# A tiled adapter with per-sequence experts: tile 0's transposes in two banks, one bias copy moved up, one weight load on another queue

## Chip, cores and metric

One core of one Trainium2 chip. The time is device microseconds of one execution; medians are over several executions. Engines: TensorE (PE), VectorE (DVE), ScalarE (ACT), GpSimd (POOL) and SyncE (SP).

## What is computed

64 sequences of 64 rows and 512 columns (float32) go through an adapter. Each sequence chooses one of three experts by an index. The reference, cut:

```python
h = jnp.einsum('bsh,bhk->bsk', x, W_down[stream]) + b_down[stream]   # 512 -> 256
h = gelu(h)
h = jnp.einsum('bsk,bkh->bsh', h, W_up[stream]) + b_up[stream]       # 256 -> 512
h = x + h
out = layernorm(h) * ln_w[stream] + ln_b[stream]
```

## The kernel before

**Tiles.** Sequences are sorted by expert on the chip and packed in pairs: 33 tiles of 128 rows. `t` is the tile; buffers go by `t` modulo 2 (`PAR`), 4 (`DEEP`, `YBANKS`) or 8 (`FAR`).

**Split products.** Each float32 operand is split into a high part (a cast to float32r by ScalarE) and a low part (operand minus high part, by VectorE or GpSimd). A product is three matmul passes: high by high, high by low, low by high. So a tile takes these steps: PE transposes x into a PSUM bank (`transpose_x`, 4 transposes); ACT casts it (`x_hi`), DVE subtracts (`x_lo`); PE runs `down` (12 matmuls); DVE adds the bias (`down_bias`), ACT does `gelu`; PE transposes g, ACT and DVE split it (`g_hi`, `g_lo`); PE runs `up` (6 matmuls of 512 columns). POOL makes x plus the up bias (`add_bias`, into `xb`), ACT copies that into the PSUM bank `y_ps` of the tile (`seed`) before `up` adds to it; for tile 0 DVE adds it afterwards (`add_first`). Then follow the norm's steps (DVE `stats`, `mean_var`, `variance`, `scale`; POOL `power`, `shift`; ACT `rescale`) and the two stores.

**Weights.** W_up lies in three slots of two halves, each half 128x512. SP asks for each (`load_w_up`), ACT casts it (`wu_high`), and the low part (`w_up_low(slot, half)`) is made by DVE for (0,0), (0,1), (1,0) and (2,1), by POOL for (1,1) and (2,0). For tiles 1 and 2 `up` runs high by high, then low g by high weight, then high g by low weight, and waits for the low parts of DVE and POOL before the last.

**Order.** There is no planner: every engine has its own instruction order, written out by hand for the first tiles, then a loop. SP, before the change: first halves of tiles 0 and 1, W_up slot 0, tile 2, slot 1, tiles 3 and 4, slot 2, tile 5, the norm's weights, tile 6, the norm's biases, then the rest. ACT asks for the second halves of tiles 0 and 1. PE's head: transposes of tile 0, first pass of `down` 0, transposes of tile 1, other passes of `down` 0, `down` 1, transposes of g 0, of tile 2, `up` 0, then from tile 1 on g transposes, `down` of the next tile, x transposes, `up`. The bias rows come out of PSUM banks too: `y_ps[0]` holds those of expert 0 until ACT has copied them (`keep_up_bias(0)`, which signals `bu_ready`).

The lines that matter: 416 to 422 (POOL's order), 545 to 570 (ACT's), 786 to 805 (DVE's), 906 to 929 and 968 (PE).

Of the kernel before, what the change touches and what calls it, by code (L numbers as in the profile page):

```python
# [21 lines left out]
P = 128  # L22
# [3 lines left out]
def adapter_program(nc, x, itok, w_down, b_down, w_up, b_up, ln_w, ln_b, out):  # L26
# [34 lines left out]
    LATE = 10  # L61

    CLOSER = 6

    DVE_LOWS, POOL_LOWS = (2, 3, 4), (0, 1, 2)

# [3 lines left out]
    with ExitStack() as ctx:  # L70
# [6 lines left out]
        def sem(name):  # L77
            return ctx.enter_context(nc.semaphore(name))
# [109 lines left out]
        xT_ready = sem("xT_ready")  # L188
        xhi_ready = sem("xhi_ready")
        xlo_ready = sem("xlo_ready")  # L190
        h_ready = sem("h_ready")
        hb_ready = sem("hb_ready")
        g_ready = sem("g_ready")
# [22 lines left out]
        def ds(start, n):  # L216
            return bass.ds(start, n)
# [6 lines left out]
        def landed_count(t, c):  # L224

            return 32 * (t // FAR + 1) if isinstance(t, int) else t * (32 // FAR) + 32 - (32 // FAR) * (c % FAR)
# [30 lines left out]
        def load_w_up(eng, slot, e):  # L257

            for k in range(KB):
                part = w_up[ds(e, 1), k * P:(k + 1) * P, :].rearrange("a p n -> p (a n)")  # L260
                eng.dma_start(wu[:, slot, k, :], part).then_inc(wu_in[slot * KB + k], 16)
# [15 lines left out]
        def _(sp):  # L277
# [34 lines left out]
            def slot_expert(slot, reg):  # L312

                return sp.snap(reg, min_val=0, max_val=E - 1 - slot) + slot
# [12 lines left out]
            sp.reg_load(io_regs, io_table[0:1, 6:9])  # L327
            load(2, 2, rows(io_regs[:2]))
            load_w_up(sp, 1, slot_expert(1, io_regs[2]))
            sp.reg_load(head_regs[:3], io_table[0:1, 9:12])  # L330
            load(3, 3, rows(head_regs[:2]))
            load(4, 4, entries(4, 0, 2))
            load_w_up(sp, 2, slot_expert(2, head_regs[2]))
            load(5, 5, entries(5, 0, 2))
            sp.dma_start(lnw_rows[:], rows_of(ln_w, P)).then_inc(lnw_in, 16)
            load(6, 6, entries(6, 0, 2))
# [23 lines left out]
        def _(pool):  # L360
# [24 lines left out]
            def add_bias(t, c):  # L385

                e = expert_of(pool, t)
                pool.wait_ge(x_in[c % FAR], landed_count(t, c))
                if isinstance(t, int) and t == DEEP:
                    pool.wait_ge(seeded_first, 1)  # L390
                elif from_tile(t, DEEP):
                    pool.wait_ge(seeded, t - DEEP)
                pool.tensor_tensor(xb[:, c % DEEP, :], x_sb[:, c % FAR, :], bu_rows[:, ds(e * H, H)],  # L393
                                   ALU.add).then_inc(xb_ready, 1)
# [19 lines left out]
            pool.wait_ge(bu_last_ready, 1)  # L414
            pool.wait_ge(bu_ready, E - 1)
            add_bias(0, 0)
            add_bias(1, 1)
            pool.wait_ge(wu_lo_ready, KB)
            add_bias(2, 2)
            w_up_low(pool, 1, 1).then_inc(wu_lo_pool, 1)  # L420
            add_bias(3, 3)
# [33 lines left out]
        def _(act):  # L455
# [27 lines left out]
            def x_hi(t, c):  # L483

                act.wait_ge(xT_ready, t + 1)
                act.copy(xT_hi[:, c % PAR, :], xT_ps[c % PAR][:]).then_inc(xhi_ready, 1)  # L486
# [11 lines left out]
            def seed(t, c):  # L498

                act.wait_ge(xb_ready, t + 1)  # L500
                if from_tile(t, YBANKS):
                    act.wait_ge(scaled_ready, t - YBANKS + 1)
                act.copy(y_ps[c % YBANKS][:], xb[:, c % DEEP, :]).then_inc(seeded, 1)  # L503
# [41 lines left out]
            wd_high(2)  # L545
            keep_up_bias(0)
            keep_up_bias(1)
            x_hi(0, 0)
            keep_down_bias(0)
            keep_down_bias(1)  # L550
            x_hi(1, 1)
# [7 lines left out]
            wu_high(1, 1)  # L559
            g_hi(1, 1)  # L560
            seed(1, 1)
            x_hi(3, 3)
            gelu(2, 2)
            wu_high(2, 0)
            g_hi(2, 2)
            wu_high(2, 1)
            seed(2, 2)
            x_hi(4, 4)
            gelu(3, 3)
            seed(3, 3)  # L570
# [58 lines left out]
        def _(dve):  # L629
# [80 lines left out]
            def x_lo(t, c):  # L710

                dve.wait_ge(xhi_ready, t + 1)
                dve.tensor_tensor(xT_lo[:, c % PAR, :], xT_ps[c % PAR][:], xT_hi[:, c % PAR, :].bitcast(F32),  # L713
                                  ALU.subtract).then_inc(xlo_ready, 1)
# [70 lines left out]

            dve.wait_ge(up_spread, E)
            dve.tensor_copy(bu_rows[:, (E - 1) * H:E * H], y_ps[E - 1][:]).then_inc(bu_last_ready, 1)  # L787
            x_lo(0, 0)
            x_lo(1, 1)
            dve.wait_ge(bd_ready, len(bd_banks))  # L790
            down_bias(0, 0, first_experts[0])
# [72 lines left out]
        def _(pe):  # L864
# [41 lines left out]
            def transpose_x(t, c):  # L906
# [3 lines left out]
                    mm = pe.transpose(xT_ps[c % PAR][:, k * P:(k + 1) * P], x_sb[:, c % FAR, k * P:(k + 1) * P], ident[:])  # L910
                mm.then_inc(xT_ready, 1)

            def down(t, c, e, passes=(0, 1, 2)):

                w0 = e * (KH * BN)
                pe.wait_ge(xhi_ready, t + 1)
                h = h_ps[c % PAR]
                products = (xT_hi, wd_hi), (xT_hi, wd_lo), (xT_lo, wd_hi)
                for x_half, w_half in [products[i] for i in passes]:
                    if isinstance(t, int) and t == 0 and w_half is wd_lo:  # L920
                        pe.wait_ge(wd_lo_ready, E)
                    if x_half is xT_lo:
                        pe.wait_ge(xlo_ready, t + 1)
                    for k in range(KH):
                        mm = pe.matmul(h, x_half[:, c % PAR, k * P:(k + 1) * P], w_half[:, ds(w0 + k * BN, BN)],  # L925
                                       start=(w_half is wd_hi and x_half is xT_hi and k == 0),
                                       stop=(x_half is xT_lo and k == KH - 1))
                if passes[-1] == 2:
                    mm.then_inc(h_ready, 1)
# [35 lines left out]
            pe.reg_load(next_regs, up_down[0:1, 1:4])  # L965
            e_next, e_up, e_down = [pe.snap(reg, min_val=0, max_val=E - 1) for reg in next_regs]
            warm_up(WARM_UPS[2], xT_ps[1])
            transpose_x(0, 0)
            pe.wait_ge(wd_hi_ready, E)
            down(0, 0, e_first, (0,))  # L970
            transpose_x(1, 1)
# [60 lines left out]
```

## Time and profile before

| | us |
|---|---|
| median of 3 runs | 135.11 (134.45 to 135.38) |
| profiled execution | 134.34 |
| its span from first to last instruction | 132.6 |
| PE busy | 124.7 (94%) |
| DVE busy | 112.6 (85%) |
| POOL busy | 105.1 (79%) |
| ACT busy | 85.2 (64%) |

The profile is that of one execution. Busy times of PE are modelled; the loads of its weights (PEld) tell better when it went on. The mean granted clock over the span was 0.995 of full speed. A tile takes 3.48 us in the middle of the run.

### The profile page before, as it was taken

The numbers are of one execution on the slowest core, as the hardware profiler recorded it, in microseconds if no ns is written. First come the engines' busy times: TensorE is split into PE (matmuls) and PEld (weight loads), VectorE is DVE, ScalarE is ACT, GpSimd is POOL, SyncE is SP. The second block draws the span as 40 slices with busy tenths as digits, with TensorE's granted clock in tenths as the row PEclk, the third lists the DMA queues.
The fourth block names the chain that finished last, engine by engine and source line by source line (L and its number), as shares of the span: only waits on it lengthen the run. The fifth ranks groups of instructions, "written<-read, shape, count | busy, mean of one in ns | idle before, by whom it ended". The sixth has DMA issues, their size and how long they took to land.

```text
span 132.6 us, 4067 instructions
## 1 busy us (share of the span) xinstructions
PE 124.7 (94%) x846; PEld 112.5 (85%) x847; DVE 112.6 (85%) x276; ACT 85.2 (64%) x179; POOL 105.1 (79%) x119
## 2 busy tenths in 40 slices
PE   6996999999999999999999999999999999999950
PEld 6885899999999999999999999999999999998730
DVE  1987897988879989888888888988888988888996
ACT  0867778577665787666666667666666666666620
POOL 7002588999879988988888888888888899988861
PEclk9999999999999999999999999999999999999998
DMA  1968869994566545556555555555555665331385
GB/s 35 333 208 267 245 170 307 274 278 163 161 182 154 142 128 161 159 157 158 158 158 143 150 150 155 158 158 158 158 158 158 158 158 119 77 70 26 69 237 161
DMA packets 13249, 21.95 MB, mean 166 GB/s; under 512 B 2345, under 2 KB 3890, under 8 KB 13234
## 3 DMA queue, kind: packets, MB, share of 16 engines
q1 hardware_dynamic: 8850, 15.74, 41.2%
q10 hardware_dynamic: 4384, 6.05, 17.0%
q14 instruction: 11, 0.09, 0.2%
q8 instruction: 4, 0.07, 0.2%
HBM read 13.39 MB, written 8.65 MB: 166 GB/s over the span
## 4 chain that ended last, share of the span: by engine, by line
PE 83%; DVE 8%; DMA 4%; issue 1%; DVEq 1%; ACT 0%; SPq 0%
PE hg_ps L925 35%; PE y_ps L958 32%; PE xT_ps L910 11%; PE hg_ps L935 5%; DMA x_sb<-in_x_dram 2%; DMA itok_all_i<-in_itok_B_dram 2%; DVE r_stats L733 1%; DVE res L782 1%; DVE y_ps L773 1%; DVEq L694 1%; DVE hb L721 1%; DVE scaled L760 1%; ACT xT_hi L486 0%; DVE r_mv L737 0%; DVE res L768 0%
## 5 line engine op out<-in xcount | busy, mean ns | idle before, releaser
L393 POOL TENSOR_TENSOR xb<-x_sb,bu_rows 128x512 f32<-128x512 f32 x33 | 42.6, 1293 | 11.1 <-DVE bu_rows L787 9.4
L410 POOL TENSOR_TENSOR res<-normed,lnb_rows 128x512 f32<-128x512 f32 (+1 forms) x31 | 39.2, 1267 | 8.4 <-ACT normed L511 8.1
L491 ACT ACTIVATE g<-hb 128x256 f32<-128x256 f32 x33 | 13.8, 419 | 32.2 <-DVE hb L721 32.1
L733 DVE BATCH_NORM_STATS2 r_stats<-y_ps 128x6 f32<-128x512 f32 x33 | 22.9, 694 | 3.1 <-issue 2.3
L925 PE MATMUL hg_ps<-wd_hi,xT_hi 128*128 x132 | 23.7, 301 | 0.9 <-ACT xT_hi L486 0.9
L713 DVE TENSOR_TENSOR xT_lo<-xT_ps,xT_hi 128x512 fp32r<-128x512 f32 x33 | 22.7, 687 | 1.9 <-ACT xT_hi L486 1.8
L958 PE MATMUL y_ps<-wu_hi,gT_hi 128*128 (+1 forms) x66 | 23.3, 433 | 0.6 <-ACT gT_hi L496 0.5
L760 DVE SCALAR_TENSOR_TENSOR scaled<-y_ps,r_mv,lnw_rows 128x512 f32<-128x512 f32 x31 | 23.0, 744 | 0.4 <-issue 0.2
L511 ACT ACTIVATE normed<-scaled,rstd 128x512 f32<-128x512 f32 x31 | 22.5, 724 | 0.0
L399 POOL TENSOR_TENSOR rstd<-var_eps,half_neg 128x1 f32<-128x1 f32 x33 | 18.0, 547 | 4.3 <-DVE var_eps L742 4.2
L925 PE MATMUL hg_ps<-wd_lo,xT_hi 128*128 x132 | 21.2, 283 | 0.0
L925 PE MATMUL hg_ps<-wd_hi,xT_lo 128*128 x132 | 21.0, 281 | 0.0
L958 PE MATMUL y_ps<-wu_hi,gT_lo 128*128 (+1 forms) x66 | 20.9, 398 | 0.0
L958 PE MATMUL y_ps<-wu_lo,gT_hi 128*128 (+1 forms) x66 | 20.7, 395 | 0.0
L486 ACT CAST xT_hi<-xT_ps 128x512 fp32r<-128x512 f32 x33 | 18.8, 573 | 2.5 <-PE xT_ps L910 2.4
L910 PE MATMUL xT_ps<-ident,x_sb 128*128 128x128 f32 x132 | 19.7, 273 | 0.5 <-DMA x_sb<-in_x_dram 0.5
L721 DVE TENSOR_TENSOR hb<-hg_ps,bd_rows 128x256 f32<-128x256 f32 x33 | 14.0, 423 | 6.2 <-PE hg_ps L925 5.3
L503 ACT COPY y_ps<-xb 128x512 f32<-128x512 f32 x32 | 18.9, 590 | 0.1
L925 PEld LDWEIGHTS hg_ps<-wd_hi,xT_hi 128*128 128x128 f32 x132 | 17.8, 189 | 1.2 <-issue 1.1
L925 PEld LDWEIGHTS hg_ps<-wd_lo,xT_hi 128*128 128x128 f32 x132 | 17.9, 188 | 0.0
L925 PEld LDWEIGHTS hg_ps<-wd_hi,xT_lo 128*128 128x128 f32 x132 | 17.9, 188 | 0.0
L910 PEld LDWEIGHTS xT_ps<-ident,x_sb 128*128 128x128 f32 x132 | 15.2, 140 | 0.7 <-DMA x_sb<-in_x_dram 0.7
(89 smaller groups left out, 149.5 us busy)
## 6 DMA issues: line engine op xcount, KB each, us to landing
x_sb<-in_x_dram SPq DMA_DIRECT2D x64, 128.0 KB, 2.7
out_dram<-res ACTq DMA_DIRECT2D x33, 128.0 KB, 2.3
out_dram<-res SPq DMA_DIRECT2D x33, 128.0 KB, 2.3
wd<-in_L_cond_W_down_dram ACTq DMA_DIRECT2D x3, 512.0 KB, 4.8
wu<-in_L_cond_W_up_dram SPq DMA_DIRECT2D x6, 256.0 KB, 3.4
lnw_rows<-in_L_cond_ln_w_dram SPq DMA_DIRECT2D x1, 768.0 KB, 5.7
lnb_rows<-in_L_cond_ln_b_dram SPq DMA_DIRECT2D x1, 768.0 KB, 7.1
x_sb<-in_x_dram ACTq DMA_DIRECT2D x2, 128.0 KB, 2.6
```

The source lines that it names most:

```text
L393: pool.tensor_tensor(xb[:, c % DEEP, :], x_sb[:, c % FAR, :], bu_rows[:, ds(e * H, H)], ALU.add).then_inc(xb_ready, 1)
L399: pool.tensor_tensor(rstd[:, c % DEEP:c % DEEP + 1], var_eps[:, c % DEEP:c % DEEP + 1], half_neg[:], ALU.pow).then_inc(rstd_ready, 1)
L410: pool.tensor_tensor(res[:, c % FAR, part], normed[:, c % DEEP, part], lnb_rows[:, ds(e * H, part.stop)], ALU.add).then_inc(res_ready, 1)
L486: act.copy(xT_hi[:, c % PAR, :], xT_ps[c % PAR][:]).then_inc(xhi_ready, 1)
L503: act.copy(y_ps[c % YBANKS][:], xb[:, c % DEEP, :]).then_inc(seeded, 1)
L511: act.activation(normed[:, c % DEEP, :], scaled[:, c % DEEP, :], ACT.Copy, scale=rstd[:, c % DEEP:c % DEEP + 1]).then_inc(normed_ready, 1)
L713: dve.tensor_tensor(xT_lo[:, c % PAR, :], xT_ps[c % PAR][:], xT_hi[:, c % PAR, :].bitcast(F32), ALU.subtract).then_inc(xlo_ready, 1)
L733: dve.bn_stats(r_stats[:, c % DEEP, :], y_ps[c % YBANKS][:]).then_inc(stats_ready, 1)
L760: dve.scalar_tensor_tensor(out=scaled[:, c % DEEP, :], in0=y_ps[c % YBANKS][:], scalar=r_mv[:, c % DEEP, 0:1], in1=lnw_rows[:, ds(e * H, H ...
L910: mm = pe.transpose(xT_ps[c % PAR][:, k * P:(k + 1) * P], x_sb[:, c % FAR, k * P:(k + 1) * P], ident[:])
L925: mm = pe.matmul(h, x_half[:, c % PAR, k * P:(k + 1) * P], w_half[:, ds(w0 + k * BN, BN)], start=(w_half is wd_hi and x_half is xT_hi and ...
L958: mm = pe.matmul(y_ps[c % YBANKS][:], g_half[:, c % PAR, k * P:(k + 1) * P], w_half[:, ds(w0 + k * H, H)], start=(unseeded and n == 0 and ...
```

## The change

1. Tile 0's four transposes are split: two go to the first half of `xT_ps[0]`, two to the second half of `y_ps[0]`, after the bias rows have been copied out of it. ACT casts the halves one after the other and signals each; DVE subtracts in two steps, after both casts; `down` 0 waits for the first half, and before its third matmul for the second.
2. On ACT `seed(2, 2)` stands ahead of `x_hi(3, 3)`.
3. W_up's slot 2 is asked for by POOL, after `add_bias(0, 0)`. The wait for the low parts of slot 0 then stands ahead of `add_bias(1, 1)`, where it was behind it. On SP the two issues go.

```diff
@@ sync @@
-            sp.reg_load(head_regs[:3], io_table[0:1, 9:12])
+            sp.reg_load(head_regs[:2], io_table[0:1, 9:11])
             load(3, 3, rows(head_regs[:2]))
             load(4, 4, entries(4, 0, 2))
-            load_w_up(sp, 2, slot_expert(2, head_regs[2]))
             load(5, 5, entries(5, 0, 2))
@@ gpsimd @@
             add_bias(0, 0)
+            slot_reg = pool.alloc_register("slot2")
+            pool.reg_load([slot_reg], io_table[0:1, 11:12])
+            load_w_up(pool, 2, pool.snap(slot_reg, min_val=0, max_val=0) + 2)
+            pool.wait_ge(wu_lo_ready, KB)
             add_bias(1, 1)
-            pool.wait_ge(wu_lo_ready, KB)
             add_bias(2, 2)
             w_up_low(pool, 1, 1).then_inc(wu_lo_pool, 1)
@@ scalar @@
-            x_hi(0, 0)
+            act.wait_ge(x0_first, 1)
+            act.copy(xT_hi[:, 0, 0:HALF], xT_ps[0][:, 0:HALF]).then_inc(x0_hi_first, 1)
+            act.wait_ge(xT_ready, 1)
+            act.copy(xT_hi[:, 0, HALF:], y_ps[0][:, HALF:]).then_inc(xhi_ready, 1)
@@
             seed(1, 1)
+            seed(2, 2)
             x_hi(3, 3)
             gelu(2, 2)
             wu_high(2, 0)
             g_hi(2, 2)
             wu_high(2, 1)
-            seed(2, 2)
             x_hi(4, 4)
@@ vector @@
-            x_lo(0, 0)
+            dve.wait_ge(xhi_ready, 1)
+            dve.tensor_tensor(xT_lo[:, 0, 0:HALF], xT_ps[0][:, 0:HALF], xT_hi[:, 0, 0:HALF].bitcast(F32), ALU.subtract)
+            dve.tensor_tensor(xT_lo[:, 0, HALF:], y_ps[0][:, HALF:], xT_hi[:, 0, HALF:].bitcast(F32),
+                              ALU.subtract).then_inc(xlo_ready, 1)
@@ tensor @@
+            def transpose_first():
+
+                pe.wait_ge(x_in[0], landed_count(0, 0))
+                for k in range(KH // 2):
+                    mm = pe.transpose(xT_ps[0][:, k * P:(k + 1) * P], x_sb[:, 0, k * P:(k + 1) * P], ident[:])
+                mm.then_inc(x0_first, 1)
+                pe.wait_ge(bu_ready, 1)
+                for k in range(KH // 2, KH):
+                    mm = pe.transpose(y_ps[0][:, k * P:(k + 1) * P], x_sb[:, 0, k * P:(k + 1) * P], ident[:])
+                mm.then_inc(xT_ready, 1)
@@ down @@
-                pe.wait_ge(xhi_ready, t + 1)
+                first = isinstance(t, int) and t == 0
+                pe.wait_ge(x0_hi_first, 1) if first else pe.wait_ge(xhi_ready, t + 1)
@@
+                        if first and k == KH // 2:
+                            pe.wait_ge(xhi_ready, 1)
@@
-            transpose_x(0, 0)
+            transpose_first()
```

## Rows read from the trace of the kernel before

**Rows 1.** The page's engine table: busy us, share, instructions.
```profile
PE 124.7 (94%) x846; PEld 112.5 (85%) x847; DVE 112.6 (85%) x276; ACT 85.2 (64%) x179; POOL 105.1 (79%) x119
```

**Rows 2.** Busy by stretch: PE, PEld, DVE, ACT, POOL, PE clock, DMA share, GB/s.
```profile
50.00:100.00 50.00, 50.00 (x349) 45.49 (x348) 44.07 (x102) 33.92 (x74) 43.99 (x43) 1.00 0.55 154
```

**Rows 3.** The chain that ended last, 10 to 13 us: start, us, what.
```profile
10.23 0.67 PE xT_ps L910 x4
...
10.92 0.59 ACT xT_hi L486
11.52 0.24 issue
11.76 0.77 PE hg_ps L925 x4
```

**Rows 4.** Order of time, PE: the first two transposes of tile 0.
```profile
10.23 0.44 PE L910 MATMUL xT_ps<-ident,x_sb 128*128 128x128 f32 x2 [0.47 <-DMA x_sb<-in_x_dram]
```

**Rows 5.** Order of time, ScalarE, 13 to 23 us.
```profile
13.48 1.14 ACT L516 CAST wu_hi<-wu 128x512 fp32r<-128x512 f32 x2
14.68 0.42 ACT L491 ACTIVATE g<-hb 128x256 f32<-128x256 f32 x1
15.83 0.37 ACT L496 CAST gT_hi<-hg_ps 128x256 fp32r<-128x256 f32 x1 [0.74 <-PE hg_ps L935]
...
17.58 0.62 ACT L516 CAST wu_hi<-wu 128x512 fp32r<-128x512 f32 x1
...
20.05 0.59 ACT L486 CAST xT_hi<-xT_ps 128x512 fp32r<-128x512 f32 x1 [1.00 <-PE xT_ps L910]
...
22.45 0.60 ACT L503 COPY y_ps<-xb 128x512 f32<-128x512 f32 x1
```

**Rows 6.** Order of time, PE's weight loads, 15 to 21 us.
```profile
15.31 0.25 PEld L935 LDWEIGHTS hg_ps<-ident,g 128*128 128x128 f32 x2
15.53 0.47 PEld L910 LDWEIGHTS xT_ps<-ident,x_sb 128*128 128x128 f32 x4
16.25 0.30 PEld L958 LDWEIGHTS y_ps<-wu_hi,gT_hi 128*128 128x128 f32 x2 [0.26 <-ACT gT_hi L496]
...
20.08 0.42 PEld L958 LDWEIGHTS y_ps<-wu_hi,gT_lo 128*128 128x128 f32 x2
20.54 0.42 PEld L958 LDWEIGHTS y_ps<-wu_lo,gT_hi 128*128 128x128 f32 x2
```

**Rows 7.** Order of time, VectorE, 14 to 20 us.
```profile
14.56 1.07 DVE L272 TENSOR_TENSOR wu_lo<-wu,wu_hi 128x512 fp32r<-128x512 f32 x1
15.56 0.68 DVE L272 TENSOR_TENSOR wu_lo<-wu,wu_hi 128x512 fp32r<-128x512 f32 x1
...
17.71 0.88 DVE L272 TENSOR_TENSOR wu_lo<-wu,wu_hi 128x512 fp32r<-128x512 f32 x1
18.51 0.69 DVE L749 TENSOR_TENSOR y_ps<-y_ps,xb 128x512 f32<-128x512 f32 x1
19.11 0.41 DVE L727 TENSOR_TENSOR gT_lo<-hg_ps,gT_hi 128x256 fp32r<-128x256 f32 x1
```

**Rows 8.** GpSimd, 13 to 20 us, and its register loads: ns min/median/max.
```profile
13.79 1.30 POOL L393 TENSOR_TENSOR xb<-x_sb,bu_rows 128x512 f32<-128x512 f32 x1
16.74 1.29 POOL L393 TENSOR_TENSOR xb<-x_sb,bu_rows 128x512 f32<-128x512 f32 x1 [1.66 <-DVE wu_lo L272]
18.28 1.47 POOL L272 TENSOR_TENSOR wu_lo<-wu,wu_hi 128x512 fp32r<-128x512 f32 x1 [0.24 <-ACT wu_hi L516]
...
L221 POOLq TENSOR_LOAD <-tile_expert x3: 288/288/511, 11.8 to 16.3; - x3
```

**Rows 9.** SP: slot 0's second issue, tile 2's second; after each, issue to landing.
```profile
9.81 0.36 SPq L261 DMA_DIRECT2D wu<-in_L_cond_W_up_dram  x1
...
DMA to landing us min/median/max: 2.9/3.5/4.1
...
11.74 0.47 SPq L255 DMA_DIRECT2D x_sb<-in_x_dram  x1
...
DMA to landing us min/median/max: 3.6/3.6/3.6
```

More of the change, by code:

```diff
@@ L63, in adapter_program @@
     CLOSER = 6
+    HALF = H // 2
     DVE_LOWS, POOL_LOWS = (2, 3, 4), (0, 1, 2)
@@ L190, in adapter_program @@
         xlo_ready = sem("xlo_ready")
+        x0_first = sem("x0_first")
+        x0_hi_first = sem("x0_hi_first")
         h_ready = sem("h_ready")
```

## Prediction

> **What bounds it now.** I read the page's engine table first, then the busy time by stretch, the chain that ended last, and last each engine's order of time from 10 to 23 us, where all the edits lie. The first two say that TensorE (PE) is the bound: 94% busy over the span, and without a gap at full clock from 50 to 100 us [rows 1, 2]. So time is won only where PE waits before that, or in the tail, which the change does not touch; and a wait won early is kept only if no other engine holds PE up afterwards. The chain shows the wait that the first edit aims at [rows 3]: four transposes of tile 0 from 10.23, ScalarE's cast for 0.59, 0.24 of "issue" on PE, then the first down matmul at 11.76. From there on the chain stays on PE, but that hides waits of a tenth or three of a microsecond that are covered by the modelled ends of matmuls. The weight loads (PEld) show when PE really goes on, and I use them below.
>
> I write s for how much earlier than before PE is. The question is how much of the s won at 11.76 is left at 21 us.
>
> **Edit 1, tile 0 in two banks.** The first two transposes are over at 10.23 + 0.44 = 10.67 [rows 4]. ScalarE takes up PE's end within 0.02 us [rows 3] and casts half a tile; the nearest row is its 128x256 cast out of PSUM, 0.37 [rows 5]: 10.69 to 11.06. With the same 0.24 of issue the first matmul starts at 11.30, so s = 0.46. The other two transposes still end at 10.90; their cast runs from about 10.95 to 11.32. The third matmul would start about 0.25 after the first, at 11.55. If the second wait costs another 0.24 after 11.32, it starts at 11.56. I take s = 0.45, with 0.40 as the low end if both halves of the cast run worse than the row. The wait on the bias copy out of the borrowed bank costs nothing: that copy is ScalarE's work before the casts and over before the transposes. VectorE's subtraction becomes two of about 0.41 (as its 128x256 row [rows 7]) that overlap a little, some 0.06 longer; PE asks for the result about 0.4 later, so that lies beside other work.
>
> **What is late next, first time.** The second half of W_up's first slot is asked for at 9.81 and needs 4.1, so it lands at 13.91 [rows 9]. ScalarE's cast of it started at 13.48 + 1.14 - 0.62 = 14.00 [rows 5], which was only 0.09 after that. It can start at 13.95 now and no sooner. The gelu of tile 0 follows 0.52 behind (the distance of those two casts' starts), 14.47 to 14.89, and PE's load of g, at 15.31 before, comes at 14.94 and not at 14.86 [rows 5, 6]. s falls to 0.37. The transposes of tile 2 wait for a load asked for at 11.74 that takes 3.6 and lands at 15.34 [rows 9]; before they began at 15.53 [rows 6], so they move by 0.15 only. For PE this is hidden: they take 0.43, up(0) could go at 15.81, and the cast of g's transpose lets it go at 16.25 - 0.37 = 15.88 anyway. But ScalarE's work behind those transposes (the cast of tile 2, gelu 1, the casts of slot 1) moves by 0.15 and not by 0.37.
>
> **Edit 3, slot 2 asked on GpSimd (POOL).** In SP's queue two issues and a register load go; the loads of x and of the two norm vectors behind them start about 2 us earlier, and none of them is waited for. On POOL the queue was: add_bias 0 and 1, wait for two low parts, add_bias 2, low part (1,1). Now it is: add_bias 0, a register load, two DMA issues, the wait, add_bias 1, add_bias 2, low part (1,1). So after the wait one more pass of 1.29 stands ahead of low part (1,1), for which PE waits in up(1). Against this, the wait ends earlier. VectorE's first low part took 1.07 where the second took 0.68 [rows 7]: it stood still while POOL was in add_bias 1, which ended at 13.79 + 1.30 = 15.09 [rows 8]; 14.56 + 1.07 - 0.68 = 14.95, so the hold ends 0.14 before POOL's end. The same shows at 17.71 (0.88, held by add_bias 2 that ended at 18.03) and, the other way about, in POOL's 1.47 at 18.28, held by VectorE until about 18.46 [rows 7, 8]. An op of two SBUF inputs and a POOL pass exclude each other. With add_bias 1 out of the way and VectorE 0.45 ahead, the two low parts end at 14.56 - 0.45 + 0.60 + 0.68 = 15.39, where 0.60 is the distance at which such ops follow each other. POOL's next pass began 0.50 after the wait was met (16.24 to 16.74), so add_bias 1 can begin at t = 15.89.
>
> That holds if the two issues are done by then. They begin when add_bias 0 ends, at 13.82, so each may take D = 1.03. No row has a DMA issued by POOL. Bounds: 0.36, the same transfer's issue on SP [rows 9], and 1.30, a whole 128x512 pass on POOL [rows 8]. POOL's first register load took 0.51 against 0.29 for the later ones [rows 8], so a first use there costs some tenths. I take the middle, 0.83, which hides; the upper end is kept for the range.
>
> The Trainium skill ("SBUF — State Buffer", the trap box on SWDGE and the section "Who interferes with whom") says more against this edit: descriptors of a DMA issued by GpSimd are written by its own cores, which are locked out while VectorE runs in a 2-port mode, and such a DMA should go to the ACT or SP queue. It adds that a tensor_tensor holds only the read side, by inference. By the strict reading the two issues would end only after VectorE's low parts (the third rival below, some 135.2 to 135.8), by the lenient one they would not be touched, and the sum below stands.
>
> **What is late next, second time.** With t = 15.89, add_bias 2 runs 17.14 to 18.43. VectorE's low part (1,0) needs ScalarE's cast, so it asks at 17.71 - 0.15 = 17.56, is held until 18.31 and ends at 18.99 instead of 18.59. Behind it on VectorE stand add_first, 0.69 [rows 7], from 18.91 to 19.60, and g_lo 1, 19.51 to 19.92 (19.52 before). PE's second pass of up(1) needs g_lo 1: its load was at 20.08 and would be at 19.71, but comes at 19.97. That is a stall of 0.26, s = 0.11. Low part (1,1) gets the port at 18.87 and ends at 20.16; PE wants it at 20.54 - 0.11 = 20.43 [rows 6], covered by 0.27.
>
> **Edit 2, tile 2's bias copy moved up.** It stood behind the cast of tile 3 and two more ops and ended at 22.45 + 0.60 = 23.05 [rows 5]. It now waits for add_bias 2 (18.43) and stands ahead of the cast of tile 3, which waited for PE until 20.05 [rows 5]. It fits between bias copy 1 and that cast. It gains nothing by itself, and takes away a wait that would bite once s is above about 0.1 at up(2). If add_bias 2 came after 19.3, gelu 2 would be late.
>
> **Sum.** 0.45 - 0.08 - 0.26 = 0.11 of gain: the profiled execution of 134.34 us (span 132.6 and 1.74 around it) becomes 134.23. The median shown is 0.77 above that execution, so the median forecast is 135.0.
>
> **Rivals.**
> - Full gain. VectorE gets the port before add_bias 2 does, or g_lo 1 is not late for another reason. Then s = 0.37 stays, 133.97 or a median of 134.7. For it: PE's slack before low part (1,1). Against it: three rows fit the exclusion within 0.02.
> - POOL's issues are long. Beyond D = 1.24, t = 13.82 + 2D is after 16.3, and VectorE takes the port between add_bias 1 and 2 while both of POOL's later ops shift. Low part (1,1) then ends at t + 4.28, PE needs it at 20.12, and s = 16.21 - t. At D = 1.30 that is -0.2, a median of 135.3. It is slower than before from D = 1.2 and slower by 1% (1.35 us, t = 17.6) from D = 1.9. Nothing in the trace has such a price, but nothing has the operation either.
> - The issues are shut out by VectorE's low parts. One issue gets through before 14.11, the other starts at 15.27, ends at about 16.1 if D is 0.83, and t = 16.1 gives add_bias 2 the port until 18.5, g_lo 1 at 20.2 and s = -0.1: median 135.2. If both wait, t = 16.9, s = -0.7: 135.8.
> - The change doesn't do what it says, because transfers are late: the two that bind (13.91, 15.34) are in the sum, but slot 2 now moves beside slot 1's second half. Up(1) would only feel that if it slipped by over 0.5; then s is about -0.2, 135.3.
>
> **How the numbers follow.** Forecast (s from 0 to 0.25) 0.45; full gain 0.17; long issues 0.2, a quarter of it beyond 1%; shut out 0.1; late transfers 0.08. A measurement of this kernel tells about 1%, 1.35 us, from no change. The full gain is a third of that, so faster by over 1% has 0.03 for scatter alone. Slower has 0.05 for long issues and 0.04 for what a third queue may cost around the span, which no row shows: 0.09. Same has 0.88. The range runs from the full gain less 0.4 of scatter (the runs lie 0.9 apart) to both issues shut out plus 0.3: 134.3 to 136.1.
>
> **What would show it.** First down matmul at about 11.3; PE's load of g 0 near 14.94; two DMA issues on POOL after 13.82 with their D; add_bias 1 at about 15.9 and add_bias 2 at about 17.1; a low part (1,0) on VectorE longer than 1 us; PE's load for the second pass of up(1) near 19.97; then every later step about 0.1 earlier. It is wrong if up(1) runs 0.37 early, if D is above 1.24, or if the time around the span is no longer 1.7.

## The result and the profile after

| | before | after |
|---|---|---|
| median of 22 runs each, us | 135.07 (134.37 to 136.12) | 135.9 (134.69 to 138.47) |
| profiled execution, us | 134.34 | 135.66 |
| its span, us | 132.6 | 133.9 |

The changed kernel takes 1.0052 of the time before, 95% interval [1.0029, 1.0074]: it is slower, by less than 1%. All ratios here leave out executions over 1.5% above the fastest of the same kernel, which are five of the changed kernel's (136.75 to 138.47 us) and none of before's; the medians of all 22 stand at 1.006. No set of runs of before has one over 136.5 us. Four of the five long ones show a mean granted clock of 0.979 to 0.983. The profiles of e4 and e11 (the changed kernel again) are of such long executions, at 0.979, and show the same wait at a larger size with a stretch at the lower clock behind it.

The engine table of the changed kernel stands beside [rows 1]: nearly the same work in a span that is 1.3 us longer.

```profile
PE 124.7 (93%) x846; PEld 112.4 (84%) x847; DVE 113.0 (84%) x277; ACT 85.1 (64%) x180; POOL 106.6 (80%) x121
```

So some engine waited. The waits of TensorE in the changed kernel, 9 to 40 us (us in total, times, longest; L922 is the transposes from tile 1 on, L929 those of tile 0):

```profile
PE xT_ps L922 <- DMA x_sb<-in_x_dram: 1.2, 1, 1.2
PE hg_ps L951 <- ACT xT_hi L555: 0.4, 1, 0.4
PE xT_ps L929 <- DMA x_sb<-in_x_dram: 0.4, 1, 0.4
```

The weight loads of the changed kernel in order of time place the first one:

```profile
11.69 0.43 PEld L951 LDWEIGHTS hg_ps<-wd_hi,xT_hi 128*128 128x128 f32 x3 [0.67 <-issue]
...
15.20 0.25 PEld L961 LDWEIGHTS hg_ps<-ident,g 128*128 128x128 f32 x2
...
16.15 0.30 PEld L984 LDWEIGHTS y_ps<-wu_hi,gT_hi 128*128 128x128 f32 x2 [0.26 <-ACT gT_hi L502]
...
20.65 0.42 PEld L922 LDWEIGHTS xT_ps<-ident,x_sb 128*128 128x128 f32 x4 [1.40 <-DMA x_sb<-in_x_dram]
21.04 0.30 PEld L984 LDWEIGHTS y_ps<-wu_hi,gT_hi 128*128 128x128 f32 x2
```

In this execution everything ahead of tile 0's transposes ran 0.37 later than in before (they began at 10.60, against 10.23 in [rows 3]). With that taken off, TensorE's lead s is 11.76 + 0.37 - 11.69 = 0.44 at the first down matmul, 0.48 at the load of g 0 (15.31 in [rows 6]) and 0.47 at up(0) (16.25 in [rows 6]). Then TensorE stands still at tile 3's transposes, and up(1) comes at 21.04. The loads of before at the same two places:

```profile
19.31 0.46 PEld L910 LDWEIGHTS xT_ps<-ident,x_sb 128*128 128x128 f32 x4
19.74 0.30 PEld L958 LDWEIGHTS y_ps<-wu_hi,gT_hi 128*128 128x128 f32 x2
```

So up(1) is 1.30 later, or s = -0.93. That 1.30 is the whole difference of the two spans; 0.37 of it is the late start of this one execution, which e11, the same kernel, does not have (tile 0's transposes at 10.02), and 0.93 is the kernel's. The tile's row tells what was late. It is tile 3's second half, asked for on SP's queue (first line its issue, ns; below who waited for it, us):

```profile
L259 SPq DMA_DIRECT2D x_sb<-in_x_dram x1: 469/469/469, 15.2 to 15.2; - x1
...
  PEld xT_ps L922: 1.4, 1
  PE xT_ps L922: 1.2, 1
  POOL xb L396: 0.3, 1
...
DMA to landing us min/median/max: 5.5/5.5/5.5
```

In before the same transfer was asked for at 14.9 and landed after 2.8, and nothing waited for it:

```profile
L255 SPq DMA_DIRECT2D x_sb<-in_x_dram x1: 468/468/468, 14.9 to 14.9; - x1
...
DMA to landing us min/median/max: 2.8/2.8/2.8
```

The stretches, after first and before behind (columns as in [rows 2]; the last two are the DMA engines' share and GB/s), show what lay beside it:

```profile
17.00:18.00 1.00, 1.00 (x8) 0.83 (x7) 0.87 (x2) 1.00 (x3) 1.00 (x2) 1.00 0.93 322
18.00:19.00 1.00, 1.00 (x11) 1.00 (x10) 1.00 (x1) 1.00 (x4) 1.00 (x2) 1.00 1.03 328
```

```profile
17.00:18.00 1.00, 1.00 (x7) 0.78 (x7) 0.87 (x2) 1.00 (x3) 1.00 (x1) 1.00 0.39 133
18.00:19.00 1.00, 1.00 (x11) 1.00 (x10) 1.00 (x2) 1.00 (x3) 0.76 (x2) 1.00 0.72 156
```

The DMA engines were full where they had been at 0.4 to 0.7. GpSimd and VectorE did what was forecast. GpSimd of the changed kernel, then VectorE:

```profile
14.21 1.35 POOL L265 DMA_DIRECT2D wu<-in_L_cond_W_up_dram  x2
16.29 2.56 POOL L396 TENSOR_TENSOR xb<-x_sb,bu_rows 128x512 f32<-128x512 f32 x2 [0.72 <-DVE wu_lo L276]
18.80 1.72 POOL L276 TENSOR_TENSOR wu_lo<-wu,wu_hi 128x512 fp32r<-128x512 f32 x1
```

```profile
14.48 1.28 DVE L276 TENSOR_TENSOR wu_lo<-wu,wu_hi 128x512 fp32r<-128x512 f32 x2
...
17.61 1.78 DVE L276 TENSOR_TENSOR wu_lo<-wu,wu_hi 128x512 fp32r<-128x512 f32 x1
19.31 0.69 DVE L758 TENSOR_TENSOR y_ps<-y_ps,xb 128x512 f32<-128x512 f32 x1
19.91 0.41 DVE L736 TENSOR_TENSOR gT_lo<-hg_ps,gT_hi 128x256 fp32r<-128x256 f32 x1
```

The two issues took 1.35 together (0.79 and 0.56), the low part (1,0) was held to 1.78, and g_lo 1 ended at 20.32. That would have held up the second pass of up(1), but TensorE was then still waiting for tile 3.

### The profile page after: what moved, and what is told of

Read it like the earlier page. It is cut to its first block, busy times and chain, and to the rows that moved or that the text cites. A ratio compares the mean times of both kernels' runs of the same rounds, so it can differ in the third digit from the quotient of the medians.

```text
span 133.9 us, 4069 instructions
## 1 busy us (share of the span) xinstructions
PE 124.7 (93%) x846; PEld 112.4 (84%) x847; DVE 113.0 (84%) x277; ACT 85.1 (64%) x180; POOL 106.6 (80%) x121
## 3 DMA queue, kind: packets, MB, share of 16 engines
q10 hardware_dynamic: 4384, 6.05, 16.5%
## 4 chain that ended last, share of the span: by engine, by line
PE 76%; DMA 6%; DVE 5%; SPq 5%; POOL 3%; issue 2%; ACT 1%; POOLq 0%; ACTq 0%; DVEq 0%
PE hg_ps L951 31%; PE y_ps L984 30%; PE xT_ps L922 10%; PE hg_ps L961 5%; DMA x_sb<-in_x_dram 4%; DMA itok_all_i<-in_itok_B_dram 2%; SPq L259 2%; POOL res L413 2%; SPq L265 1%; DVE res L791 1%; DVE y_ps L782 1%; POOL rstd L402 1%; SPq L331 1%; ACT normed L517 0%; DVE r_stats L742 0%
## 5 line engine op out<-in xcount | busy, mean ns | idle before, releaser
L497 ACT ACTIVATE g<-hb 128x256 f32<-128x256 f32 x33 | 13.8, 418 | 32.5 <-DVE hb L730 32.4
L722 DVE TENSOR_TENSOR xT_lo<-xT_ps,xT_hi 128x512 fp32r<-128x512 f32 x32 | 22.0, 688 | 2.3 <-ACT xT_hi L492 2.3
L402 POOL TENSOR_TENSOR rstd<-var_eps,half_neg 128x1 f32<-128x1 f32 x33 | 18.1, 548 | 4.4 <-DVE var_eps L751 4.2
L984 PE MATMUL y_ps<-wu_lo,gT_hi 128*128 (+1 forms) x66 | 20.6, 393 | 0.0
L492 ACT CAST xT_hi<-xT_ps 128x512 fp32r<-128x512 f32 x32 | 18.2, 570 | 3.4 <-PE xT_ps L922 3.3
L922 PE MATMUL xT_ps<-ident,x_sb 128*128 128x128 f32 x128 | 19.1, 273 | 1.2 <-DMA x_sb<-in_x_dram 1.2
L730 DVE TENSOR_TENSOR hb<-hg_ps,bd_rows 128x256 f32<-128x256 f32 x33 | 13.9, 422 | 6.0 <-PE hg_ps L951 4.9
L951 PEld LDWEIGHTS hg_ps<-wd_hi,xT_lo 128*128 128x128 f32 x132 | 18.1, 188 | 0.0
L922 PEld LDWEIGHTS xT_ps<-ident,x_sb 128*128 128x128 f32 x128 | 14.7, 140 | 1.4 <-DMA x_sb<-in_x_dram 1.4
```

Of the source, the lines that this page charges most:

```text
L402: pool.tensor_tensor(rstd[:, c % DEEP:c % DEEP + 1], var_eps[:, c % DEEP:c % DEEP + 1], half_neg[:], ALU.pow).then_inc(rstd_ready, 1)
L984: mm = pe.matmul(y_ps[c % YBANKS][:], g_half[:, c % PAR, k * P:(k + 1) * P], w_half[:, ds(w0 + k * H, H)], start=(unseeded and n == 0 and ...
```

## The experiments

All of them compute the whole result; e8 makes two small transfers and e14 one fill besides that nothing reads. Two theories stood against each other at first. Traffic: slot 2's 0.52 MB, asked for about 3 us earlier and on another queue, makes tile 3's x late. Order: the moved wait and the third queue cost the time on GpSimd, whatever is transferred.

**Which edit costs: e1, e2, e4.** e1 undoes edit 3. e2 undoes only its transfers and keeps the early wait. e4 is before with edit 3 alone. The differences to the changed kernel and to before:

```diff
# e1: changed kernel; on SP load_w_up(sp, 2, ...) stands again; on POOL
-            load_w_up(pool, 2, ...)
-            pool.wait_ge(wu_lo_ready, KB)
             add_bias(1, 1)
+            pool.wait_ge(wu_lo_ready, KB)
# e2: as e1, but the wait stays ahead of add_bias(1, 1)
# e4: before; on POOL
             add_bias(0, 0)
+            load_w_up(pool, 2, ...)
+            pool.wait_ge(wu_lo_ready, KB)
             add_bias(1, 1)
-            pool.wait_ge(wu_lo_ready, KB)
```

> Edits 1 and 2 alone: slot 2 is asked on SP behind tile 4 and the wait for the low parts stands behind add_bias 1, as before. In the changed kernel tile 3's transposes waited 1.2 us for their x, whose second half took 5.5 us from issue to landing where it took 2.8 before; by up(0) it had been 0.47 ahead of before. Traffic theory (slot 2's 0.52 MB now moves beside tile 3's load): tile 3's x takes about 2.9 again and the kernel is 0.3 to 0.45 us faster than before, ratio about 0.997. Queue theory (a transfer asked on GpSimd slows the others by its own way): the same. Port theory (up(1) is late because add_bias 2 holds VectorE's low part): the same. If the late x came from edit 1, ratio 1.005 as the changed kernel.

> Edits 1 and 2, and of edit 3 only the order on GpSimd (the wait for the low parts ahead of add_bias 1); slot 2 is asked on SP as before. Tells the port theory from the two on transfers. Port theory, as I had forecast it: low part (1,0) on VectorE takes over 1 us, add_first and g_lo 1 come late, PE's load for the second pass of up(1) comes 0.2 to 0.3 late, and the gain is 0.1 to 0.2 us less than that of edits 1 and 2 alone: ratio 0.998 to 1.000. Traffic and queue theory: tile 3's x is in time (about 2.9 us), so no 1.2 us wait; 0.1 us faster than before at least.

> Edit 3 alone on the kernel before. Traffic and queue theory: tile 3's x lands as late as in the changed kernel, so PE waits about 0.75 to 1.2 us and nothing of edit 1's 0.45 stands against it: ratio 1.007 to 1.010. If the edits only hurt together (tile 3 wanted 0.45 earlier), ratio about 1.003. Bias copy 2 stands behind wu_high(2,1) here as before, which costs nothing as long as PE is that late.

Measured: e1 1.0038 [1.0012, 1.0063], e2 1.0027 [0.9996, 1.0058], e4 1.0095 [1.0058, 1.0131]. In e1 and e2 tile 3's halves land after 2.7 to 3.7 us and nothing waits for them. In e4 the second half, asked for at 14.7, takes 6.7 us and TensorE's weight loads stand still for 2.03. So edit 3 brings the wait without edits 1 and 2, and e2 shows that its early wait alone does not. Edit 3 also lets SP ask for tile 5's x and the norm's weights sooner (18.1 and 19.3 in the changed kernel, 19.4 and 20.6 in before). No run moves these without slot 2, so a share of theirs in the delay is not excluded. By their ratios alone e1 and e2 can't be told from the changed kernel; what tells them apart is the traces and the long runs, none of 12 in each. The windows of e4 add what a wait of that size draws after it (columns as in [rows 2]; the seventh value is the granted clock):

```profile
20.00:21.00 1.00, 0.00 (x0) 0.00 (x0) 0.83 (x3) 0.00 (x0) 0.69 (x1) 1.00 1.00 291
21.00:22.00 1.00, 0.54 (x3) 0.54 (x4) 0.00 (x0) 0.00 (x0) 0.42 (x1) 0.78 1.05 283
22.00:23.00 1.00, 1.00 (x5) 0.90 (x4) 0.00 (x0) 0.43 (x1) 0.85 (x1) 0.50 1.01 309
...
24.00:25.00 1.00, 1.00 (x4) 0.66 (x3) 0.48 (x1) 0.00 (x0) 0.95 (x1) 0.52 0.98 238
25.00:26.00 1.00, 1.00 (x11) 1.00 (x10) 0.25 (x1) 0.65 (x2) 0.91 (x4) 1.00 1.05 281
```

TensorE did nothing from 20 to 21, and from 21.6 to 25 it was granted the lower of its two levels (1.2 and not 2.4 GHz). up(1) begins 2.29 late and up(2) 3.60 late against before, each counted from tile 0's transposes, so the lower clock added 1.3 to the wait. In the 1.2 us wait of the changed kernel the clock stayed at 1.00. That is how one late load becomes 0.5% in one execution and over 2% in another (e4's profiled execution took 138.34).

e2 shows the forecast stall, and one that was not forecast. Its weight loads around up(1):

```profile
20.26 0.30 PEld L982 LDWEIGHTS y_ps<-wu_hi,gT_lo 128*128 128x128 f32 x2 [0.33 <-DVE gT_lo L734]
20.63 0.40 PEld L982 LDWEIGHTS y_ps<-wu_lo,gT_hi 128*128 128x128 f32 x2
21.48 0.20 PEld L959 LDWEIGHTS hg_ps<-ident,g 128*128 128x128 f32 x2 [0.45 <-ACT g L495]
```

The 0.45 is put down to gelu 2, but that had ended at 20.99. What ran until about 21.4 was the load of TensorE's registers for tile 2, which its queue issues behind up(1). The rows of that line, e2 and then before (ns min/median/max, first and last start us):

```profile
L908 PEldq TENSOR_LOAD <-up_down x30: 533/549/960, 20.8 to 121.4; - x30
```

```profile
L898 PEldq TENSOR_LOAD <-up_down x30: 535/547/969, 20.1 to 120.6; - x30
```

In before the queue runs ahead and the load of 0.54 lies under matmuls. After the stall of e2 it starts 0.7 later (0.25 of that is e2's later start) and lies open.

e1's gain went in another way: tile 1's x took 4.0 us to land, TensorE's load for its transposes waited 0.20, and s fell from .35 to .13. Its profile (span 132.5) shows no loss, so its 1.0038, most of what the changed kernel lost, is not explained. Edit 1 without the bias copy came out at 0.9983 and 0.9994 (e5, e16 below); one kernel timed in two sets of runs differs by about 0.0012 (e5 and e16, after and e11), which is too little to explain it.

**Each small edit alone: e5, e6, e16.** e5 is edit 1 alone, e16 the same kernel once more, and e6 edit 2 alone.

```diff
# e5, e16: before with the two-bank transposes, casts and subtractions of tile 0
# e6: before with
             seed(1, 1)
+            seed(2, 2)
             x_hi(3, 3)
```

> Edit 1 alone (tile 0 in two banks). In the profile of edits 1 and 2, s was 0.35 at the first down matmul and only 0.13 from tile 1's transposes on, which waited for their x (4.0 us to landing); its median was nevertheless 0.4% above before. Cap theory: early transfers (x of tiles 1 and 2, W_up's first slot) cap the gain at 0.1 to 0.2 us whatever PE wins at tile 0: ratio 0.998 to 1.001. Edit 2 costs theory: the loss of edits 1 and 2 comes from bias copy 2 standing ahead of tile 3's cast, so edit 1 alone is faster, ratio 0.997, and edit 2 alone slower. Full gain, as I had forecast for this part by itself: 0.997.

> Edit 2 alone (bias copy 2 ahead of the cast of tile 3). By the trace of before, add_bias 2 ends at 18.03 and ScalarE is free until 20.05: cost and gain zero, ratio 0.999 to 1.001. Edit 2 costs theory: where x of tile 2 is late, add_bias 2 is late too, and it now holds the cast of tile 3 and gelu 2: ratio 1.002 to 1.004.

> Edit 1 alone once more, to see how steady its ratio and its place are. Theory that the gain of edit 1 hangs on when tile 0's x lands against the bias copy on ScalarE: first down matmul 0.1 to 0.5 earlier than before, most of it lost in up(0) to VectorE's held low parts, ratio 0.997 to 1.000. Rival, that its 0.9983 was chance: ratio 1.000 to 1.003.

Measured: e5 0.9983 [0.9956, 1.0011], e16 0.9994 [0.9958, 1.0029], e6 1.0013 [0.9978, 1.0048]. None can be told from no change. e5's trace shows edit 1's gain won and lost, VectorE first and then the weight loads of up(0):

```profile
14.33 2.10 DVE L276 TENSOR_TENSOR wu_lo<-wu,wu_hi 128x512 fp32r<-128x512 f32 x2
```

```profile
16.02 0.30 PEld L982 LDWEIGHTS y_ps<-wu_hi,gT_hi 128*128 128x128 f32 x2 [0.26 <-ACT gT_hi L500]
16.49 0.30 PEld L982 LDWEIGHTS y_ps<-wu_lo,gT_hi 128*128 128x128 f32 x2 [0.17 <-DVE wu_lo L276]
17.15 0.30 PEld L982 LDWEIGHTS y_ps<-wu_hi,gT_lo 128*128 128x128 f32 x2 [0.37 <-DVE gT_lo L734]
```

With add_bias 1 still in its old place GpSimd holds the two low parts to 2.10 (1.28 in the changed kernel), and up(0) gives back 0.17 and 0.37. e16 shows 2.17, 0.24 and 0.37. So by these traces edit 1 needs the early wait to keep its gain through up(0); no ratio is fine enough to show it.

**How much traffic, on which queue, and when: e3, e7, e8, e11, e12, e14.**

```diff
# e3: changed kernel, slot 2 asked on ScalarE's queue
-            load_w_up(pool, 2, ...)      # POOL, behind add_bias(0, 0)
             gelu(0, 0)                   # ACT
+            load_w_up(act, 2, ...)
# e7: half 0 of slot 2 on POOL, half 1 on SP at its old place
# e8: slot 2 on SP at its old place; on POOL two transfers of 4 KB
+                pool.dma_start(scratch[:, k * 8:(k + 1) * 8], part)
# e11: the changed kernel again
# e12: changed kernel, wait for the low parts behind add_bias(1, 1) again
# e14: changed kernel with 0.52 us of other work ahead of the two issues
+            pool.memset(scratch[:], 0.0)
             load_w_up(pool, 2, ...)
```

> The changed kernel with slot 2 asked on ScalarE's queue (behind gelu 0, about 14.7 and 15.2 us) and not on GpSimd's (14.2 and 15.0): the same bytes at nearly the same time, another way to issue. Traffic theory: tile 3's x lands late here too, 4.5 to 5.5 us for its second half, PE waits 0.7 to 1.2 us at tile 3's transposes, ratio 1.003 to 1.006. Queue theory: tile 3's x takes about 3 us, no wait, and the time is that of the early wait alone, ratio 0.998 to 1.000.

> The changed kernel with only the first half of slot 2 (0.26 MB) asked on GpSimd, the second half on SP behind tile 4: half the dose of the early traffic. Traffic theory: tile 3's second half of x takes about 4 us to land (2.8 before, 5.5 with the whole slot), PE waits less than 0.3 us for it, and the time is that of the early wait alone, ratio 0.999 to 1.002. If the way of GpSimd's queue were all of it, one such transfer would hurt nearly as much as two: landing 5 us and more, ratio 1.004.

> Edits 1 and 2 and the early wait, slot 2 on SP as before, and two GpSimd transfers of 4 KB each into a tile that nobody reads: GpSimd's issues at the same place without the traffic. Traffic theory: tile 3's x takes about 3 us, the two issues take about 0.8 and 0.56 us on GpSimd as in the changed kernel and are over before the wait is met, ratio equal to that of the kernel with the early wait alone (1.003 with an interval from 1.000 to 1.006). Queue theory (what GpSimd does to issue or a third queue's presence hurts): tile 3's x late by over 1 us, ratio above 1.005.

> The changed kernel itself, beside the others on one chip and for a second profile: tile 3's x lands over 4.5 us after its issue again, PE waits for it, ratio 1.005 (1.003 to 1.008).

> The changed kernel with the wait for the low parts behind add_bias 1 again, so of edit 3 only the transfers on GpSimd are left. Traffic theory: the late x of tile 3 is all there is, ratio as the changed kernel's, 1.004 to 1.007, with VectorE's low parts of slot 0 held as before. Port theory for the loss: it would be near 1.000.

> The changed kernel with one fill of an unused 128x512 tile on GpSimd ahead of slot 2's two issues, which then start about 0.4 to 0.6 later, at 14.7 and 15.5, as those of e3_slot2_on_act (14.6 and 15.0) or later. Theory that the loss is traffic that lies beside tile 3's x and depends on the time of asking alone: tile 3's second half lands after 4.7 or less, PE's wait is 0.2 to 0.5, ratio 1.001 to 1.003. Rival, that transfers from GpSimd's queue press harder on those of SP's whatever their time: the second half still takes 5.3 or more, PE waits over 0.8, ratio 1.004 to 1.008.

Measured, with tile 3's two halves as time of asking + us to landing, and the wait as the idle time of TensorE's weight loads ahead of tile 3's transposes:

| kernel | slot 2 asked | tile 3's x | wait | ratio | runs over 136.5 |
|---|---|---|---|---|---|
| before | SP 17.3, 18.3 | 14.3+3.0, 14.9+2.8 | 0 | | 0 of 22 |
| e8 (8 KB) | POOL 13.8, 14.6 | 14.2+2.9, 14.9+4.2 | 0.22 | 0.9993 [0.9966, 1.0021] | 0 of 12 |
| e7 (half) | POOL 14.0 | 14.5+3.9, 15.1+4.2 | 0.19 | 1.0012 [0.9988, 1.0035] | 0 of 12 |
| e3 | ACT 14.6, 15.0 | 14.2+3.9, 14.9+4.7 | 0.38 | 1.0015 [0.9989, 1.0041] | 0 of 12 |
| e14 | POOL 14.6, 15.4 | 14.1+2.9, 14.7+3.2 | 0 | 1.0030 [1.0011, 1.0049] | 1 of 12 |
| after | POOL 14.2, 15.0 | 14.5+4.7, 15.2+5.5 | 1.40 | 1.0052 [1.0029, 1.0074] | 5 of 22 |
| e11 | POOL 13.9, 14.7 | 14.1+4.9, 14.7+6.8 | 2.55 | 1.0039 [0.9997, 1.0081] | 4 of 13 |
| e4 | POOL 13.8, 14.6 | 14.1+5.0, 14.7+6.7 | 2.03 | 1.0095 [1.0058, 1.0131] | 4 of 9 |
| e12 | POOL 14.5, 15.3 | 14.8+5.0, 15.4+6.9 | 1.18 | 1.0092 [1.0052, 1.0132] | 7 of 12 |

Three readings. First, GpSimd's issues cost nothing that shows in the time (e8), and half the bytes cost less than all. But e8's 8 KB do not leave tile 3 untouched: its second half takes 4.2 us, as with half of slot 2 in e7, where it takes 2.7 to 3.7 in the ten other profiles with all of slot 2 on SP. That is one execution, and no run follows it up, so bytes are not shown to be all of it. Second, where the first half of slot 2 is asked for on GpSimd 0.8 to 1.0 us ahead of tile 3's second half and the rest follows, that takes 5.5 to 6.9 us; where it is asked for 0.1 to 0.3 ahead, 3.2 to 4.7. Third, e14 speaks for time against queue, in one execution: tile 3 is asked for at the same times as in e11, slot 2 from the same queue but 0.7 later, and tile 3 lands nearly as before. The DMA packets in the traces fit this. Slot 2's first packet moves 1.6 to 2.0 us after its first issue on GpSimd's queue, and 1.4 after it on ScalarE's. In after, e4, e11 and e12 it moves 0.8 to 1.0 us after tile 3's second half was asked for, in e3 1.1, and in e14 only 1.6, when that half needs 1.6 more. The next in line is hit. The landing rows of e14, tile 3's second half and then tile 4's (asked for at 16.5):

```profile
DMA to landing us min/median/max: 3.2/3.2/3.2
```

```profile
DMA to landing us min/median/max: 5.8/5.8/5.8
```

Nothing waited for tile 4. So a slowness of GpSimd's queue as such, which seemed likely after e3, is not needed: the time of asking is enough. Of e14's 0.3% its trace shows the two stalls of e2 again, 0.44 for g_lo 1 and 0.46 behind it for the register load. e12 shows that the early wait was not the harm: without it the time is no better. Its profiled execution (137.42) was late from the start, tile 0's transposes at 12.1 against 10.6 in after, so only its wait of 1.18 is read from it. e11 repeats the changed kernel: its median over all 13 runs is 135.94. The medians of all runs against before's give the same order as the ratios: 1.006 for after and for e11, 1.011 for e12, 1.013 for e4, 1.003 for e14.

**Can the gain be kept: e9, e10, e13, e15.**

```diff
# e10: e2 with TensorE's registers of tile 2 loaded earlier
             transpose_x(3, 3)
+            e_up2, e_down2 = experts_from(2)
             up(1, 1, e_up)
# e9: e10 with seed(2, 2) back in its place and on POOL
             add_bias(1, 1)
             w_up_low(pool, 1, 1)
             add_bias(2, 2)
             w_up_low(pool, 2, 0)
             add_bias(3, 3)
# e13: e9 with add_bias(3, 3) ahead of w_up_low(pool, 2, 0), and on SP
             load(4, 4, ...)
+            sp.dma_start(lnw_rows[:], ...)
             load_w_up(sp, 2, ...)
             load(5, 5, ...)
-            sp.dma_start(lnw_rows[:], ...)
# e15: as e13, but lnw_rows between load_w_up(sp, 2, ...) and load(5, 5, ...)
```

> The kernel with edits 1, 2 and the early wait (slot 2 on SP), with PE's register load of tile 2's experts moved ahead of up(1). In three profiles with a stall of 0.2 to 0.35 us at the second pass of up(1), PE stood another 0.45 us before tile 2's g transposes, with ScalarE named, but that register load (0.54 us) began only at 20.6 to 20.8 us, where it began at 20.1 in the kernel before. Register theory: the 0.45 goes and the stall at the second pass (0.2 to 0.35) stays; ratio 0.3% below that of the same kernel without the move. ScalarE theory (gelu 2 is really late): the 0.45 stays.

> A kernel meant to keep edit 1's gain: edit 1, the early wait on GpSimd, slot 2 on SP as before, bias copy 2 at its old place, GpSimd's order add_bias 0, wait, add_bias 1, low part (1,1), add_bias 2, low part (2,0), add_bias 3, and PE's register load for tile 2 ahead of up(1). Port theory: neither the two low parts of slot 0 nor low part (1,0) on VectorE is held, so PE stalls neither in up(0) nor at the second pass of up(1); s stays at 0.3 to 0.45 where the transfers let it: ratio 0.996 to 0.998. Cap theory (x of tiles 1 and 2 land too late): 0.998 to 1.000. If the order makes a later add_bias late, above 1.

> Edit 1 with the early wait, slot 2 on SP behind the norm's weights (which stood behind tile 5 before), GpSimd's order: add_bias 0, wait, add_bias 1, low part (1,1), add_bias 2, add_bias 3, low part (2,0); PE's register load of tile 2 ahead of up(1); the bias copy of tile 2 at its old place. Theory that the gain of e9_low_parts_first was lost to the late norm weights and to the late add_bias 3: the norm weights are asked at about 17.4 and land before 24, PE waits for no xT_lo at 26 to 30 us, PE keeps s of 0.3 to 0.4 into the loop, span about 132.3, ratio 0.9965 to 0.9985. Rival, that a lead of PE is lost in any case at the next resource: another wait shows behind 24 us (slot 2's low part (2,0), asked at 18 and made at 22 by GpSimd, or tile 5), ratio 0.999 to 1.001.

> As e13_norm_weights_early, but the norm's weights stay behind slot 2 on SP and only change places with tile 5's x. Theory that the loss of e13 came from slot 2's transfers beside the norm's weights: slot 2 lands after 3.0 to 3.6 again, the norm's weights are asked at about 19.3 and land by 26, PE waits for nothing from 16 to 30 us and keeps s of 0.3 to 0.4, span 132.2 to 132.6, ratio 0.9965 to 0.9985. Rival, that the next transfer pays as each one did that was moved: tile 5's x, now beside the norm's weights, lands later than it is needed, or the norm weights still come too late for tile 0's scale; ratio 0.999 to 1.003.

Measured: e10 0.9982 [0.9942, 1.0021], e9 1.0005 [0.9968, 1.0043], e13 1.0409 [1.0364, 1.0454], e15 1.0003 [0.9958, 1.0049]. e10 settles the register load. Its weight loads show the wait for g_lo 1 as in e2, and none behind it:

```profile
20.19 0.30 PEld L982 LDWEIGHTS y_ps<-wu_hi,gT_lo 128*128 128x128 f32 x2 [0.44 <-DVE gT_lo L734]
20.55 0.41 PEld L982 LDWEIGHTS y_ps<-wu_lo,gT_hi 128*128 128x128 f32 x2
21.01 0.36 PEld L959 LDWEIGHTS hg_ps<-ident,g 128*128 128x128 f32 x2
```

The intervals of e10 and e2 overlap, so what this saves is read from the trace alone. e9 removes the hold of low part (1,0) too (0.69 again) and TensorE keeps s of about 0.38 through up(3), but loses it at 26 to 30 us: its weight loads stand 0.65 for xT_lo, since VectorE stands behind the norm's weights, asked for at 20.9 and 7.2 on the way. e13 was to cure that by asking for them earlier. It is the mistake of the change once more, at a far higher price (4.1% against 0.5%). Slot 2 now lies beside the norm's weights, its halves take 5.3 and 6.0, and ScalarE waits. The waits in e13, 16 to 27 us, and TensorE's weight loads:

```profile
ACT wu_hi L520 <- DMA wu<-in_L_cond_W_up_dram: 3.1, 2, 2.9
...
PE y_ps L982 <- ACT y_ps L507: 2.8, 1, 2.8
```

```profile
26.31 0.35 PEld L982 LDWEIGHTS y_ps<-wu_hi,gT_hi 128*128 128x128 f32 x2 [3.07 <-issue]
```

The bias copy of tile 2 stands behind that cast on ScalarE, so up(2) waits for it, and the clock falls to 0.50 afterwards as in e4. In e15 slot 2 lands after 3.1 and 3.0 again, and the ratio is back at 1; but 6 of its 12 runs are over 136.5, its median is 136.53 against 135.27, and its profile (span 133.2) does not show why. No version tried is measurably faster than before.

## Why the prediction was wrong

The forecast was 135.0 and a lead of 0.11 kept; it is 135.9, and slower by 0.5%. The time lies inside the range, 134.3 to 136.1, but the likeliest case and its sign were wrong, and that the range holds it is luck: it was made for other causes. By its steps:

- **Edit 1** was right at its place: 0.44 for 0.45, the first cast 0.37 for 0.37. What the forecast took as fixed moves: where tile 0's x lands early, the second pair waits for the bias copy out of the borrowed bank, 0.35 in e14 (transposes at 10.13, first down matmul at 11.63, s = 0.03) and 0.27 in e11 (10.02, 11.44, s = 0.12). That the wait on the bias copy "costs nothing" held in the profiled execution of after and not in these two, one of them the same kernel. "What is late next, first time" took 0.08 off; none of that showed in after (0.48 at g 0), where the second half of slot 0 took 3.1 to land and not 4.1.
- **D** was 0.79 and 0.56 for 0.83, hidden as forecast, and add_bias 1 began at 16.29, which is 15.89 + 0.37 and 0.03. The rival of long issues fell.
- **Shut out by VectorE** fell as well. The two low parts ran from 14.48 to 15.76 in 1.28 with an issue beside them, and the issues ran back to back in 1.35, the same as in e4 and e8. The Trainium skill ("SBUF — State Buffer", "Who interferes with whom") leaves it at an inference that a tensor_tensor does not lock the descriptor writing out; these rows agree with it. On ScalarE's queue (e3), one of the two that the Trainium skill's trap box on SWDGE names instead of GpSimd's, the wait for tile 3 was 0.38 and not 1.40; that can't be put down to the queue, since slot 2 was also asked for 0.4 later.
- **Low part (1,0)** was right in kind: 1.78 for the forecast 1.43, and a stall at the second pass of up(1) of 0.33 to 0.44 in e2, e10 and e14 for 0.26. What stood behind it was missed: the register load, another 0.45. The sum 0.45 - 0.08 - 0.26 = 0.11 becomes -0.34 with it, without any late transfer. At the load of g 2, with the later start of each execution taken off (0.25 and 0.16), s is 21.01 + 0.25 - 21.48 = -0.22 in e2, and 21.01 + 0.16 - 21.01 = 0.16 in e10, where the register load is out of the way: close to the forecast 0.11.
- **The step that failed** is a term put at nothing: the sum has no wait for tile 3's x. The rival of late transfers says that "the two that bind (13.91, 15.34) are in the sum", and laid the moved slot 2 only beside "slot 1's second half"; under edit 3 the forecast looked only at the loads behind slot 2 in SP's queue. (Of those it was right that none is waited for; they start 1.3 us earlier and not about 2.) The transfer that was moved to 14.2 was never laid against tile 3's x, asked for at 14.5 and 15.2 and wanted at 19.2. In before that x landed at 17.7, 1.6 before TensorE wanted it. A cover of 1.6 against a load time that went from 2.8 to 5.5 was the number to work out, and it was not. In its place the runs showed a wait of 1.40 in after, 2.03 in e4 and 2.55 in e11. That rival had a chance of 0.08 and s = -0.2; s was -0.93, and where the wait was 2.0 to 2.6 the clock fell on top.
- The chances: "slower by over 1%" had 0.09. The ratio (0.5%) is not there, but six of the 22 runs are over 1% above before's median.

What the Trainium skill says in "DMA: Bandwidth & Descriptors" ("Queues, rings and completion order") would have pointed there: each DMA engine takes turns between the queues that have work for it. By that rule slot 2 on a second queue shares the engines with tile 3 as soon as its packets move, where behind tiles 3 and 4 on SP's own queue it started after them. The table agrees (5.5 to 6.9 us with slot 2 on GpSimd's queue, 4.7 on ScalarE's), though e13 shows that within one queue a large transfer ahead does the same (5.3 to 6.0).

Open: why e15 has its long runs; e1's ratio; why 8 KB on GpSimd's queue went with a landing of 4.2 in e8; and what sets the exact delay, 5.5 in one execution and 6.8 in another of the same kernel.

## What to carry to other kernels

When a transfer is asked for earlier, list every load that is then in flight with it, and write down for each how long before its use it landed; here a big one asked for a microsecond ahead of a small one doubled the small one's time. A gain on the binding engine at the head must be followed through each resource it meets (VectorE held up by GpSimd, a register load, the next landing) before it is counted, and a single execution's landing times are not the margin, their spread is. A wait of 2 us on TensorE cost more than itself here, since the clock fell behind it.

## What the runs showed of the hardware

- A DMA issue on GpSimd takes 0.79 us for the first and 0.56 for the second, whether it moves 256 KB or 4 KB (1.35 for both in after, e4, e8 and e12); on SP's queue a transfer of 256 KB took 0.36 [rows 9], though slot 2's first took 0.98 in before.
- After 1.40 us without a weight load TensorE kept its clock (after); after 2.0 to 3.1 us without one (e4, e11, e13) over 3 us at the lower level followed.
- A load of TensorE's registers took 0.54 us and cost nothing where the queue ran ahead (before, e10); after a stall of 0.33 it cost 0.45 (e2).
- A 128x512 low part on VectorE took 0.69 alone and 1.78 beside two GpSimd passes (after); two GpSimd DMA issues beside two low parts held up neither (1.35 and 1.28).
- The norm's weights, 0.79 MB, took 4.8 (e13) to 7.4 us (e14) to land, with what lay beside them.
